# Graph attention in one sweep over 256 destinations

## The chip, the cores and the metric

One core of a Trainium2 chip runs the program once; the time is device microseconds of that execution. TensorE (PE) does matmuls and transposes, VectorE (DVE), ScalarE (ACT) and GpSimd (POOL) the elementwise work, SyncE (SP) issues DMAs. Tiles lie in SBUF or in PSUM (8 banks of 512 fp32 columns on 128 partitions), and the engines run apart from each other except for semaphores.

## The reference, cut to what matters

Four residual graph layers over 3125 nodes (padded to 3200 = 25 tiles of 128), 128 features and 103125 edges, each followed by a layer norm: a weighted sum with relu, the graph attention (GAT) that the change rewrites, a dot-product attention, and a two-layer mean aggregation. GAT, with 4 heads of 32 features and one self loop added per node:

```
h = (x @ W).reshape(n, HEADS, C)
a_s = jnp.einsum('nhc,hc->nh', h, att_src)
a_d = jnp.einsum('nhc,hc->nh', h, att_dst)
e = jax.nn.leaky_relu(a_s[src] + a_d[dst], NEG_SLOPE)      # slope 0.2
m = jax.ops.segment_max(e, dst, num_segments=n)
p = jnp.exp(e - m[dst])
z = jax.ops.segment_sum(p, dst, num_segments=n)
alpha = p / (z[dst] + EPS_SOFTMAX)
out = jax.ops.segment_sum(h[src] * alpha[:, :, None], dst, num_segments=n)
out = out.reshape(n, HEADS * C) + gat_bias + x @ skip_W + skip_b
```

## The kernel before

Edges are first turned into two dense 3200x3200 matrices in DRAM, rows by destination, columns by source: how often each edge occurs (`count_rs`) and the sum of its weights. `edge_tables` and `build_matrices` make them, `aggregate` and `finish_gcn` do the first layer; the change leaves these alone. Every stage is a block with its own engine programs, and the next block starts when all engines have left the one before. The order on each engine is written out by hand.

- `gat_project` computes h by head with a column of ones (`heads`), the attention terms per node (`cols`) and a_s and a_d as rows in DRAM (`rows_d`).
- `gat_max` goes over 25 tiles of 128 destinations. ScalarE sums a count tile for the degree (L941), turns it into a mask (L944, 0 where there is an edge, 1e30 where there is none) and takes its logarithm (L948). VectorE reduces a_s minus mask to a maximum for each of 4 heads (L983). TensorE turns the logarithms (L916, L917), ScalarE copies them out (L953), and they are stored as `log_sr`, rows by source.
- `gat_exponents` makes from the maximum the terms that each destination adds.
- `gat_attend` goes over the sources: 200 units of one head, one source tile and 1600 destinations. ScalarE adds a bias (L1157), VectorE takes the larger slope (L1189), then the minimum with 0 plus the log count (L1200), ScalarE raises (L1162), and TensorE gathers with the 33 columns of `heads` as stationary operand (L1214).
- `finish_gat` turns the sums back to nodes (L1272), adds each node's own loop (L1304, L1308), divides, adds the skip product, normalises twice, and turns X into XT (L485, L1295).
- `attend_rows` is the second attention, one tile of 128 destinations at a time: scores (L1435), masked minimum (L1526), Exp (L1493), times counts (L1540), turns (L1444), copies out of PSUM (L1498), gather (L1454). ScalarE masks the tile after next (L1487) in between.
- `mean_over_edges` runs twice over `log_sr`: ScalarE raises (L663), VectorE rounds to bf16 counts (L707), TensorE multiplies them with three bf16 parts of the features (L673). GpSimd copies the features (L609).

## Time and profile before

| what | us |
|---|---|
| median of 3 runs (3094.7 to 3097.13) | 3095.39 |
| the profiled execution's own time | 3097.05 |
| its span | 3095.4 |
| maximum to attend, 1108.2 to 2256.4 of the span | 1148.2 |

| | PE | DVE | ACT | POOL |
|---|---|---|---|---|
| busy us | 2427.7 | 2180.8 | 2119.9 | 579.5 |
| share of the span | 78% | 70% | 68% | 19% |

The shares are means over stages in which different engines are full, so the question for each stage is which engine never waits there. A group's row gives the busy time of its instructions as a union, their mean length, and the idle time just before them with what ended it. Two instructions on one engine can overlap, so busy time divided by the count can be less than the mean. An fp32 product leaves two MATMUL records, a transpose or a bf16 product one.

### The profile page before, as it was taken

To read this page: it belongs to the slowest core of one execution; us is meant where nothing else is said; L and a number is where in the kernel's file an instruction comes from. 1 tells how busy PE (TensorE), PEld (TensorE's weight loads), DVE (VectorE), ACT (ScalarE), POOL (GpSimd) and SP (SyncE) were. 2 spreads that over 40 slices of the span, in tenths; PEclk is the share of its full clock that TensorE was granted. 3 is DMA by queue.
4 is the path that set the end of the run, shared out by engine and by line. 5 is a ranking of instruction groups with operands and counts; after the bars stand their busy time and mean duration, and the time that the engine had idled before them with its cause. 6 is when DMAs were issued, how large, how long until landed. Compare 5 with 4: busy or idle time off the path is not lost. (4 is left out here: it accounts for less than half of the span.)

```text
span 3095.4 us, 52656 instructions
## 1 busy us (share of the span) xinstructions
PE 2427.7 (78%) x12244; PEld 1411.6 (46%) x12245; DVE 2180.8 (70%) x3601; ACT 2119.9 (68%) x3216; POOL 579.5 (19%) x950
## 2 busy tenths in 40 slices
PE   2898989999889556767488887888846999959785
PEld 1454445444445446656322222222244888845443
DVE  6777767777720249999699999999963555547165
ACT  2899989999940147777488888888824666637163
POOL 1444444444420000000011112111100000002020
PEclk7999999999999778888799999999967999979897
DMA  1222222222268047666511113111103333139093
GB/s 43 98 108 97 103 97 103 103 103 104 104 255 308 28 174 230 216 217 222 193 64 53 60 57 138 64 53 59 46 4 129 111 123 127 43 138 409 14 406 145
DMA packets 173354, 398.35 MB, mean 129 GB/s; under 512 B 7655, under 2 KB 147234, under 8 KB 156450
## 3 DMA queue, kind: packets, MB, share of 16 engines
q1 hardware_dynamic: 92698, 355.11, 31.1%
q10 hardware_dynamic: 80400, 40.96, 4.5%
q14 instruction: 233, 1.91, 0.2%
q8 instruction: 23, 0.38, 0.1%
HBM read 271.34 MB, written 124.70 MB: 128 GB/s over the span
## 5 line engine op out<-in xcount | busy, mean ns | idle before, releaser
L436 PE MATMUL ps_build<-OH,KEY 128*128 128x400 bf16 x4108 | 737.0, 339 | 82.5 <-ACT KEY L393 49.7
L393 ACT ACTIVATE KEY<-KEY,cols 128x128 bf16<-128x128 bf16 x2054 | 621.9, 397 | 98.5 <-DVE KEY L364 98.0
L1214 PE MATMUL ga_ps<-ga_p,ga_left 128*33 128x400 f32 x1600 | 567.9, 500 | 154.6 <-ACT ga_p L1162 154.6
L436 PEld LDWEIGHTS ps_build<-OH,KEY 128*128 128x128 bf16 x4108 | 399.7, 99 | 420.1 <-DVE OH L368 82.5
L364 DVE TENSOR_SCALAR KEY<-iota_key,key_base,cols 128x128 bf16<-128x128 int16 x1027 | 389.6, 412 | 219.5 <-PE ps_build L436 191.7
L411 POOL TENSOR_TENSOR KEY<-KEY,cols 128x256 bf16<-128x256 bf16 (+1 forms) x627 | 376.7, 601 | 497.8 <-DVE KEY L364 497.8
L1214 PEld LDWEIGHTS ga_ps<-ga_p,ga_left 128*33 128x33 f32 x1600 | 160.2, 110 | 562.2 <-issue 561.9
L1189 DVE SCALAR_TENSOR_TENSOR ga_p<-ga_u,att_cols,ga_p 128x1600 f32<-128x1600 f32 x201 | 376.6, 1874 | 20.2 <-ACT ga_p L1157 20.2
L1162 ACT ACTIVATE ga_p<-ga_p 128x1600 f32<-128x1600 f32 x200 | 307.3, 1536 | 95.0 <-DVE ga_p L1200 95.0
L983 DVE CUSTOM_DVE_ANT_0 gm_unread<-gm_src_rows,gm_closed 128x3200 bf16<-128x3200 f32 x100 | 343.3, 3488 | 39.2 <-ACT gm_closed L944 30.9
L1200 DVE SCALAR_TENSOR_TENSOR ga_p<-ga_p,ga_log 128x1600 f32<-128x1600 f32 x200 | 365.1, 1825 | 0.0
L1157 ACT ACTIVATE ga_p<-ga_u,att_cols 128x1600 f32<-128x1600 f32 x203 | 327.6, 1614 | 23.8 <-DMA ga_u<-gat_u_d 23.8
L1148 POOL COPY ga_left<-heads 128x33 f32 x200 | 135.5, 679 | 982.2 <-PE ga_ps L1214 571.0
L368 DVE TENSOR_SCALAR OH<-iota_low,cols 128x400 bf16<-128x400 int16 x1027 | 293.2, 317 | 0.0
L916 PE MATMUL gm_ps<-gm_minus,gm_closed 128*128 128x128 bf16 x625 | 149.9, 240 | 143.8 <-ACT gm_logs L953 120.9
L917 PE MATMUL gm_ps<-ident,gm_ring 128*128 128x128 f32 x1250 | 253.3, 340 | 0.0
L917 PEld LDWEIGHTS gm_ps<-ident,gm_ring 128*128 128x128 f32 x1250 | 223.4, 223 | 14.0
L673 PE MATMUL sage_ps<-sage_counts,sage_parts 128*128 128x400 bf16 x1200 | 206.7, 336 | 20.1 <-DVE sage_counts L707 20.1
L663 ACT ACTIVATE sage_ring<-sage_ring 128x3200 f32<-128x3200 f32 x50 | 143.5, 2871 | 62.7 <-DMA sage_ring<-log_count_by_source 62.6
L386 ACT ACTIVATE stage<-ps_build 128x800 f32<-128x800 f32 x201 | 166.2, 827 | 2.7 <-PE ps_build L436 2.6
L673 PEld LDWEIGHTS sage_ps<-sage_counts,sage_parts 128*128 128x128 bf16 x1200 | 118.3, 99 | 108.7 <-DVE sage_counts L707 21.2
L1526 DVE CUSTOM_DVE_ANT_0 ar_p<-ar_ps,ar_closed 128x1600 f32<-128x1600 f32 x50 | 91.1, 1823 | 106.1 <-PE ar_ps L1435 95.4
(287 smaller groups left out, 2414.7 us busy)
## 6 DMA issues: line engine op xcount, KB each, us to landing
adjacency<-stage SPq DMA_DIRECT2D x200, 400.0 KB, 2.5
sage_ring<-log_count_by_source SPq DMA_DIRECT2D x50, 1600.0 KB, 8.4
agg_gcn_ring<-adjacency SPq DMA_DIRECT2D x25, 1600.0 KB, 8.3
gm_ring<-adjacency SPq DMA_DIRECT2D x25, 1600.0 KB, 6.9
log_count_by_source<-gm_logs ACTq DMA_DIRECT2D x25, 1600.0 KB, 7.1
ga_log<-log_count_by_source SPq DMA_DIRECT2D x50, 800.0 KB, 4.3
ar_counts<-adjacency SPq DMA_DIRECT2D x25, 1600.0 KB, 6.7
ga_u<-gat_u_d SPq DMA_DIRECT2D x8, 1600.0 KB, 12.1
```

The source lines that it names most:

```text
L364: last = dve.tensor_scalar(KEY[:, slot + j, 0, :], k.iota_key[:, :], k.key_base[:, bass.ds(w, 1)], k.cols[:, 0, bass.ds(c + j, 1)], ALU.ad ...
L393: last = act.activation(KEY[:, slot + j, v, :], KEY[:, slot + j, 0, :], ACT.Copy, scale=k.cols[:, 1 + v, bass.ds(c + j, 1)])
L411: pool.tensor_tensor(KEY[:, slot:slot + n, 1, :], KEY[:, slot:slot + n, 0, :], k.cols[:, 2, bass.ds(c, n)].unsqueeze(2).to_broadcast([P, n ...
L436: last = pe.matmul(ps[:, 2 * (s % 2) + (v > 0), 0:SL], KEY[:, slot + j, v, :], OH[:, slot + j, :], start=slot == s % 2 * (BODY + 1) and j ...
L673: last = pe.matmul(ps[:, b, 0:CW], parts[:, u, i, :], counts[:, u, b * CW:(b + 1) * CW], start=False, stop=True, skip_group_check=True)
L917: last = pe.matmul(ps[:, b, c:c + P], ring[:, u, s * P:(s + 1) * P], k.ident[:], start=False, stop=True)
L983: dve.tensor_tensor_reduce(out=unread[:, h], in0=src_rows[:, h], in1=closed[:, u], scale=1.0, scalar=-3.0e38, op0=ALU.subtract, op1=ALU.ma ...
L1157: act.activation(p[:, slot, :], u[:, h, 1, :], ACT.Identity, bias=cols[:, HEADS + h, bass.ds(t, 1)]).then_inc(slopes, 1)
L1162: act.activation(p[:, i, :], p[:, i, :], ACT.Exp).then_inc(exps, 1)
L1189: dve.scalar_tensor_tensor(p[:, slot, :], u[:, h, 0, :], cols[:, h, bass.ds(t, 1)], p[:, slot, :], ALU.add, ALU.max).then_inc(larger, 1)
L1200: dve.scalar_tensor_tensor(p[:, slot, :], p[:, slot, :], 0.0, log[:, slot // HEADS, :], ALU.min, ALU.add).then_inc(scores, 1)
L1214: last = pe.matmul(ps[first:first + C + 1, h // 2 * HB + b, 0:CW], left[:, slot, :], p[:, slot, b * CW:(b + 1) * CW], start=False, stop=Tr ...
```

## The change

`gat_max`, `gat_exponents` and `gat_attend` become one function, `gat_rows`. It goes over 13 groups (`super_tile`) of 256 destinations, the last of 128, and in each over 4 heads: 52 units. GpSimd adds the self loops to the counts' diagonal blocks. The slope is split: e = 0.2(a_s + a_d) + max(0.8 a_s + 0.8 a_d, 0). For a unit VectorE has the masked maximum (`best`, two passes of 3125), four small steps (`level`), and `span`: for each of the two destination tiles `r = max(0.8 a_s + lift, floor)`, destinations on partitions. TensorE turns r in 50 blocks into 6 rotating PSUM banks, ScalarE raises each 128x256 block with the source's 0.2 a_s as bias (`power`), VectorE takes the minimum with 1 times the turned counts (`weigh`, 6400 columns in two parts), and TensorE gathers with 50 products of 33 stationary and 128 moving columns, the two destination tiles at PSUM partitions 0 and 64. One small product (`join`) turns a head's sums to nodes, and they go to DRAM (`node_d`). Counts are turned once per group by TensorE, copied by ScalarE and stored as `count_sr`.

`finish_gat` loads `node_d`, turns X first and no longer at its end; `attention_project` turns X instead and halves the copy between ScalarE and VectorE. The degrees are no longer a by-product of `gat_max`: ScalarE sums each count tile in `attend_rows` (`measure`), and `finish_attention` makes the reciprocal. `mean_over_edges` reads plain counts: no Exp, GpSimd subtracts the identity, VectorE casts.

```diff
+def gat_rows(nc, k, heads, cols, rows_d):
...
+            def turn_piece(g, h, i):
+                u = g * HEADS + h
+                if i == 0:
+                    pe.wait_ge(ranged, u + 1)
+                    need(pe, raised, u * PIECES)
+                    if h == 0:
+                        pe.wait_ge(taken_n, g * 5 + width(g))
+                    if h == 1:
+                        pe.wait_ge(taken_n, counts_done(g))
+                if i >= RINGS:
+                    pe.wait_ge(raised, u * PIECES + (i - RINGS + 1))
+                for s in range(i * BLOCKS, min(NT, (i + 1) * BLOCKS)):
+                    for j in range(width(g)):
+                        c = s % BLOCKS * WIDE + j * P
+                        last = pe.transpose(ps[:, i % RINGS, c:c + P], r[:, j, s * P:(s + 1) * P], k.ident[:])
+                last.then_inc(turned, 1)
...
+            def gather(g, h, s):
+                for j in range(width(g)):
+                    last = pe.matmul(ps[j * PAIR:j * PAIR + C + 1, 7, 0:P], heads[:, h, s, :], e[:, s, j * P:(j + 1) * P],
+                                     start=s == 0, stop=s == NT - 1, skip_group_check=True)
+                return last
...
+            def super_tile(g):
+                for h in range(HEADS):
+                    g0, h0 = (g, h - 1) if h else (g - 1, HEADS - 1)
+                    before = h > 0 or not is_super(g, 0)
+                    for i in range(RINGS):
+                        turn_piece(g, h, i)
+                    for i in range(RINGS, PIECES):
+                        if before:
+                            gather_chunk(g0, h0, i)
+                        turn_piece(g, h, i)
+                    if h == HEADS - 1 and not is_super(g, LAST):
+                        first_counts(g + 1)
+                    if before:
+                        join(g0, h0)
+                    gather_first(g, h)
+                    if h == 0:
+                        other_counts(g)
...
+            def power(g, h, i):
+                act.wait_ge(turned, (g * HEADS + h) * PIECES + (i + 1))
+                w = width(g) * P
+                for s in range(i * BLOCKS, min(NT, (i + 1) * BLOCKS)):
+                    c = s % BLOCKS * WIDE
+                    last = act.activation(e[:, s, 0:w], ps[:, i % RINGS, c:c + w], ACT.Exp, bias=cols[:, h, s:s + 1])
+                last.then_inc(raised, 1)
...
+            def span(g, h):
+                u = g * HEADS + h
+                need(dve, turned, u * PIECES)
+                dve.wait_ge(levelled, u + 1)
+                n = columns(g)
+                for j in range(width(g)):
+                    last = dve.tensor_scalar(r[:, j, 0:n], src_rows[:, h, 0:n], lift_u[:, h, j:j + 1],
+                                             floor_u[:, h, j:j + 1], ALU.add, ALU.max)
+                last.then_inc(ranged, 1)
+
+            def weigh(g, first, last):
+                w = width(g) * P
+                part = e[:, first:last, 0:w]
+                dve.scalar_tensor_tensor(part, part, 1.0, count_t[:, first:last, 0:w], ALU.min, ALU.mult
+                                         ).then_inc(weighed, 1)
...
+                for h in range(HEADS):
+                    span(g, h)
+                    if h:
+                        weigh_rest(g, h - 1)
+                    elif not is_super(g, 0):
+                        weigh_rest(g - 1, HEADS - 1)
+                    g2, h2 = next_best(g, h)
+                    if g2 is not None:
+                        best(g2, h2, 0)
+                    weigh_first(g, h)
+                    if g2 is not None:
+                        if width(g2) > 1:
+                            best(g2, h2, 1)
+                        level(g2, h2)
...
 def finish_gat
+            turn(pe, ps, k.X, k.ident[:]).then_inc(turned, 1)
             pe.wait_ge(copied, 1)
-            pe.wait_ge(loaded, 80)
-            project(pe, ps, [k.XT], [w[:]]).then_inc(projected, 1)
-            pe.wait_ge(x_ready, 1)
-            turn(pe, ps, k.X, k.ident[:]).then_inc(x_turned, 1)
+            pe.wait_ge(loaded, 96)
+            project(pe, ps, [XT], [w[:]]).then_inc(projected, 1)
...
 def attend_rows
+            def measure(t, u):
+                act.wait_ge(kept, t)
+                act.wait_ge(measured, t + RING)
+                act.activation(unread[:], counts[:, u, :], ACT.Copy, accum_out=deg_u[:, u % 2]).then_inc(measured, 1)
...
+                if exists(t, 2):
+                    measure(t + 2, (u + 2) % RING)
...
 def mean_over_edges
+                    pool.wait_ge(loaded[u], lap * 16 + 16)
+                    own = ring[:, u, bass.ds(t * P, P)]
+                    pool.tensor_tensor(own, own, k.ident[:], ALU.subtract).then_inc(opened, 1)
...
-                        dve.wait_ge(raised, t + 1)
-                        dve.tensor_scalar(counts[:, u, :], ring[:, u, :], ROUND, ROUND, ALU.add, ALU.subtract
-                                          ).then_inc(rounded, 1)
+                        dve.wait_ge(opened, t + 1)
+                        dve.tensor_copy(counts[:, u, :], ring[:, u, :]).then_inc(rounded, 1)
```

In the instruction order, VectorE in the attend stage before, two units (`ga_p` the exponents, `ga_u` the rows of destination terms, `ga_log` the log counts):

```order
L1188 REGISTER_ALU
L1189 ISA
L1189 SCALAR_TENSOR_TENSOR ga_p<-ga_u,att_cols,ga_p 128x1600
L1200 SCALAR_TENSOR_TENSOR ga_p<-ga_p,ga_log 128x1600
L1188 REGISTER_ALU
L1189 ISA
L1189 SCALAR_TENSOR_TENSOR ga_p<-ga_u,att_cols,ga_p 128x1600
L1200 SCALAR_TENSOR_TENSOR ga_p<-ga_p,ga_log 128x1600
```

And VectorE now, one unit of the first group of `gat_rows`, its second head:

```order
L1179 TENSOR_SCALAR gr_r<-gr_src_rows,gr_lift_u,gr_floor_u 128x3125 x2
L1186 SCALAR_TENSOR_TENSOR gr_e<-gr_e,gr_count_t 128x3328
L1152 ISA gr_unread,gr_best_u<-gr_src_rows,gr_closed 128x3125
L1152 ISA gr_best_u 128x1
L1186 SCALAR_TENSOR_TENSOR gr_e<-gr_e,gr_count_t 128x3072
L1152 ISA gr_unread,gr_best_u<-gr_src_rows,gr_closed 128x3125
L1152 ISA gr_best_u 128x1
L1162 TENSOR_TENSOR gr_peak<-gr_best_u,att_cols 128x2
L1164 SCALAR_TENSOR_TENSOR gr_peak<-gr_peak 128x2
L1167 SCALAR_TENSOR_TENSOR gr_floor_u<-gr_peak,att_cols 128x2
L1170 TENSOR_TENSOR gr_lift_u<-gr_floor_u,att_cols 128x2
```

The maximum, which had a stage of its own, now stands between the passes over the exponents, for the head after next; of the two passes with two tensors one is left, and the other is a pass with one tensor.

TensorE now, from the middle of a unit to the start of the next (`gr_r` is what is turned, `gr_e` what is gathered, `gr_out_t` what is joined); before, a unit was four products of 400 columns:

```order
L1019 MATMUL gr_ps<-gr_e,heads 33x128 x4
L990 MATMUL gr_ps<-ident,gr_r 128x128 x4
L1019 MATMUL gr_ps<-gr_e,heads 33x128 x4
L990 MATMUL gr_ps<-ident,gr_r 128x128 x4
L1019 MATMUL gr_ps<-gr_e,heads 33x128 x2
L990 MATMUL gr_ps<-ident,gr_r 128x128 x2
L1042 MATMUL gr_ps<-ident,gr_out_t 128x66
L1019 MATMUL gr_ps<-gr_e,heads 33x128 x24
L990 MATMUL gr_ps<-ident,gr_r 128x128 x24
```

Turns of one unit and products of the unit before now alternate in pieces.

ScalarE in the second attention now, from its mask to the copies of the next tile (line numbers of the changed kernel; before, the row of L1473 was not there):

```order
L1468 ACTIVATE ar_closed<-ar_counts,ar_big 128x3200
L1479 ACTIVATE ar_p<-ar_p,ar_low 128x1600 x2
L1483 REGISTER_ALU
L1484 ACTIVATE ar_pt<-ar_ps 128x512
L1483 REGISTER_ALU
L1484 ACTIVATE ar_pt<-ar_ps 128x512
L1483 REGISTER_ALU
L1484 ACTIVATE ar_pt<-ar_ps 128x512
L1483 REGISTER_ALU
L1484 ACTIVATE ar_pt<-ar_ps 128x128
L1472 REGISTER_ALU
L1473 ACTIVATE ar_unread,ar_deg_u<-ar_counts 128x3200
```

The degree's sum stands behind the last copy of a tile and ahead of the first copy of the next.

## Rows read from the trace of the kernel before

**Rows 1.** Busy time by stretch: maximum, attend, finish of GAT, second attention (columns named first).
```profile
core 0: us, PE busy (x) PEld busy (x) DVE busy (x) ACT busy (x) POOL busy (x), PEclk, DMA share, GB/s
...
1200.00:1500.00 300.00, 202.57 (x1496) 188.30 (x1496) 279.09 (x201) 227.31 (x98) 0.00 (x0) 0.84 0.67 213
...
1600.00:2200.00 600.00, 478.49 (x1354) 135.33 (x1352) 596.26 (x337) 516.48 (x338) 117.22 (x168) 0.99 0.21 68
...
2256.00:2338.00 82.00, 35.32 (x175) 34.56 (x175) 51.59 (x86) 16.75 (x35) 0.00 (x0) 0.56 0.02 4
...
2380.00:2700.00 320.00, 318.81 (x2113) 262.68 (x2111) 178.86 (x256) 214.24 (x232) 5.93 (x20) 1.00 0.30 108
```

**Rows 2.** Groups by line on VectorE: count, busy us, mean ns, idle before.
```profile
L1189 DVE SCALAR_TENSOR_TENSOR ga_p<-ga_u,att_cols,ga_p 128x1600 f32<-128x1600 f32 x201 | 376.6, 1874 | 20.2 <-ACT ga_p L1157 20.2
L1200 DVE SCALAR_TENSOR_TENSOR ga_p<-ga_p,ga_log 128x1600 f32<-128x1600 f32 x200 | 365.1, 1825 | 0.0
L983 DVE CUSTOM_DVE_ANT_0 gm_unread<-gm_src_rows,gm_closed 128x3200 bf16<-128x3200 f32 x100 | 343.3, 3488 | 39.2 <-ACT gm_closed L944 30.9 <-DVE deg L989 8.0 <-DMA gm_src_rows<-gat_rows_d 0.4
...
L243 DVE TENSOR_SCALAR pick<-win,cmin,cidx 128x200 f32<-128x200 f32 x7 | 2.7, 384 | 0.3
...
L217 DVE TENSOR_SCALAR src_hi<-src_f 128x896 f32<-128x896 f32 x1 | 0.6, 627 | 0.0
```

**Rows 3.** Groups by line on ScalarE, same columns.
```profile
L1498 ACT ACTIVATE ar_pt<-ar_ps 128x512 f32<-128x512 f32 x150 | 78.1, 591 | 79.1 <-PE ar_ps L1444 79.1
...
L941 ACT ACTIVATE gm_unread_act<-gm_ring 128x3200 bf16<-128x3200 f32 x25 | 71.8, 2871 | 83.9 <-DMA gm_ring<-adjacency 77.1 <-issue 6.0 <-ACT gm_logs L953 0.8
...
L1498 ACT ACTIVATE ar_pt<-ar_ps 128x128 f32<-128x128 f32 x25 | 7.0, 279 | 0.0
```

**Rows 4.** Groups by line on TensorE; two records stand for one fp32 product.
```profile
L1214 PE MATMUL ga_ps<-ga_p,ga_left 128*33 128x400 f32 x1600 | 567.9, 500 | 154.6 <-ACT ga_p L1162 154.6
```

**Rows 5.** Timeline of TensorE in the attend stage: start us, length us, then the group.
```profile
1700.45 2.85 PE L1214 MATMUL ga_ps<-ga_p,ga_left 128*33 128x400 f32 x8 [0.70 <-ACT ga_p L1162]
```

**Rows 6.** Timeline of one tile of the second attention.
```profile
2452.61 2.84 PE L1454 MATMUL ar_ps<-ar_pt,X 128*128 128x128 f32 x24
...
2455.28 1.47 PE L1444 MATMUL ar_ps<-ident,ar_p 128*128 128x128 f32 x12
...
2462.61 0.29 DVE L1548 COPY acc_t<-ar_ps 128x128 f32 x1 [0.52 <-PE ar_ps L1454]
2462.93 1.57 ACT L1498 ACTIVATE ar_pt<-ar_ps 128x512 f32<-128x512 f32 x3 [3.06 <-PE ar_ps L1444]
...
2466.30 2.84 PE L1454 MATMUL ar_ps<-ar_pt,X 128*128 128x128 f32 x24
...
2468.71 3.15 ACT L1493 ACTIVATE ar_p<-ar_p,ar_low 128x1600 f32<-128x1600 f32 x2 [1.36 <-DVE ar_low L1534]
```

**Rows 7.** Tile gm_ring: how long its loads took from issue to landing.
```profile
DMA to landing us min/median/max: 6.3/6.9/24.7
```

**Rows 8.** Timeline: SyncE's first load of the maximum stage.
```profile
1108.21 0.34 SPq L893 DMA_DIRECT2D gm_ring<-adjacency  x1
```

**Rows 9.** Timeline from the end of the attend stage to the second attention's projection.
```profile
2256.39 0.34 SPq L1260 DMA_DIRECT2D fg_w<-in_L_gnn_skip_W_dram  x1
...
2256.44 21.57 PE L1272 MATMUL fg_ps<-ident,head_sums 97*128 97x66 f32 x100 [3.18 <-PEq L1076]
...
2293.88 3.49 DVE L1316 TENSOR_TENSOR fg_t<-fg_t,fg_ps 128x3200 f32<-128x3200 f32 x1
...
2328.21 5.59 PE L485 MATMUL fg_ps<-ident,X 128*128 128x128 f32 x25 [38.59 <-DVEq L1321]
...
2340.48 7.54 PE L1347 MATMUL ap_ps<-XT,ap_wq 128*128 128x400 f32 x16 [6.67 <-DMA ap_wk<-in_L_gnn_Wk_dram]
```

**Rows 10.** Timeline of the start of the first mean over edges.
```profile
2766.30 2.87 ACT L663 ACTIVATE sage_ring<-sage_ring 128x3200 f32<-128x3200 f32 x1 [5.87 <-DMA sage_ring<-log_count_by_source]
...
2771.08 14.15 PE L673 MATMUL sage_ps<-sage_counts,sage_parts 128*128 128x400 bf16 x73 [9.23 <-DVE sage_counts L707]
```

More of the change, by code:

```diff
@@ new lines, in is_super, with width, columns, each_super @@
+        def is_super(g, which):
+            return isinstance(g, int) and g == which
+        def width(g):
+            return 1 if is_super(g, LAST) else TWO
+        def columns(g):
+            return NP if is_super(g, LAST) else N
+        def each_super(eng, work):
+            work(0)
+            with eng.Fori(1, LAST - 1) as g:
+                work(g)
+            work(LAST - 1)
+            work(LAST)
+        def next_best(g, h):
+            if h < TWO:
+                return g, h + TWO
+            return (None if is_super(g, LAST) else g + 1), h - TWO
@@ L889, in _, with counts_done @@
+        def counts_done(g):
+            return g * 5 + (2 * width(g) + 1)
         @block.sync
         def _(sp):
[L891 to L898 removed]
@@ L899, in _, with load, store_node @@
-            load(1, 1, 0)
-            with sp.Fori(1, NT // 2) as lap:
-                for u in range(2):
-                    load(lap * 2 + u, u, lap)
-            load(NT - 1, 0, NT // 2)
+            def load(g, j):
+                sp.dma_start(count[:, j, :].unsqueeze(1), rows[bass.ds(g * TWO + j, 1)].rearrange("t p c -> p t c")
+                             ).then_inc(loaded[j], 16)
+            def store_node(g, h):
+                n = width(g) * (C + 1)
+                hold(sp, kept, g * HEADS + (h + 1), held_sp)
+                sp.dma_start(k.node_d[:, h, bass.ds(g * (TWO * (C + 1)), n)], node[:, h % TWO, 0:n]
+                             ).then_inc(node_stored[h % TWO], 16)
@@ L1006, in gat_exponents, with finish_gat @@
+            for h in range(TWO):
+                for j in range(TWO):
+                    best(0, h, j)
+                level(0, h)
+            each_super(dve, super_tile)
+            weigh_rest(LAST, HEADS - 1)
+def finish_gat(nc, k):
     with ExitStack() as ctx:
```

678 lines of the change are left out of this document (296 added, 382 removed).

## The prediction

> **What bounds the kernel now.** I read the busy times by stretch first, to find the engine that never waits in each stage that the change touches [rows 1]. From 1200 to 1500 us (the maximum) VectorE is busy 279.09 of 300 us. From 1600 to 2200 (the attend stage) it is busy 596.26 of 600, TensorE 478.49 and ScalarE 516.48. So VectorE sets the time of both stages that are replaced, from the first load at 1108.21 [rows 8] to the first load of the next block at 2256.39 [rows 9]: 1148.2 us. The groups by line say what VectorE does there [rows 2]: 100 passes of 3200 for the maximum (343.3 us) and 401 passes of 1600 (376.6 and 365.1 us). In the second attention (2380 to 2700) TensorE is busy 318.81 of 320 [rows 1], so whatever makes TensorE wait there costs its full length. In the finish of GAT (2256 to 2338) no engine is full: a chain, read from the timeline [rows 9]. Below, a unit is one head of one group of 256 destinations, and T its period; 48 units have full width, 4 half.
>
> **VectorE's work in a unit.** A pass with two tensors costs 1.04 ns an element, from (3488 - 1825) / 1600, and 0.16 us fixed [rows 2]; queued behind another, 0.08 of that is hidden (337 instructions of mean 1.85 in 596.26 us, 1.77 each [rows 1, 2]).
> - Maximum: 343.3 / 100 is 3.43 us a pass of 3200, so 3.35 for 3125; two are 6.7 us. This work only moves: 100 passes before and after.
> - Minimum and times counts: 6400 elements in two passes, 6.67 + 2 x 0.08 = 6.8 us.
> - `span`, two passes with one tensor and two scalars per partition. No row has 3125 of them, so I bound it. A single-tensor pass of 896 took 627 ns, that is 0.52 ns an element over the same 0.16 us, half the price of two tensors. One of 200 with two such scalars took 384 ns, 0.10 + 0.28 [rows 2]. That gives 3125 x 0.52 + 0.28 = 1.9 us a pass, 3.6 for two with the overlap. The upper bound is full price, 3125 x 1.04 + 0.28 = 3.5 us a pass, or 3.1 us more a unit. I take 1.9: both rows with one tensor lie there (at full price 896 elements would have taken 1.09 us).
> - `level`: four tiny steps, each waiting for the one before: 0.9 us, the fixed 0.16 to 0.28 each.
>
> Together 18.0 us a unit. For all of the work that is some 930 us where the two stages had 1085.
>
> **TensorE's work in a unit.** At full clock (0.99 to 1.00 where TensorE was busy 80% and more [rows 1]) 24 records of 128 columns ran in 2.84 us, 12 turns in 1.47 us [rows 6]; less the last one's tail that is 0.111 us a record or turn, 0.222 a product. 50 turns are 5.55 us, 50 products 11.1, the join 0.2. That is 16.9, with 1.4 for a fourth of the count turns 18.3: the same as VectorE. To this come waits that the order forces. The join needs a copy that ScalarE makes after its last block, about 1 us after the last turn; for the last head the next group's counts are turned in that gap. After the first head, 26 count turns wait for a copy of 1536 columns (1.4 us), and the second head's turns wait for the last one. Head by head I get 21.7, 18.0, 18.0 (VectorE's) and 19.6 us, T = 19.3.
>
> ScalarE: 25 blocks of 256 between 279 ns (128 columns) and 591 ns (512) [rows 3], so about 0.38 us plus the bias, 25 x 0.46 = 11.5 at most; count copies 1.7, masks 1.5, the two small copies 0.5. Even at 591 ns a block it has 18.5 us, so it is hidden; if not, the sixth block comes late for `weigh_first`. GpSimd has only the diagonal adds. Loads: 6.9 us each [rows 7], two a group, due a unit later. The stores of counts and sums queue on SyncE behind the loads and have three units' time. If they blocked, the mask would be late and VectorE with it.
>
> **The stage.** At the start six transfers queue: 6.9 us for the first, some 4.1 for each further one (the longest landing, 24.7, was that of a load behind four others of its size [rows 7], part of it while the first was under way). So the second count tile is there at 15 us, its mask at 19, four passes and two levels follow, and the first `span` ends at 35. The last group is half wide, but its products are not paired and its first unit still gathers the wide one before: 46 us, and a tail of 8 with the sums' store. Narrow or missing passes take 10 off. So the stage takes 79 + 48 T = 1005 us against 1148.2: -143.
>
> **The rest.**
> - Finish of GAT: before, 21.57 us of products lie ahead of everything, and the add of the skip product starts 37.5 us after the block's start [rows 9]. Now the node sums (1.7 MB) and five small loads land at about 9.5 us, VectorE has 12.5 us of work, and TensorE (turns 5.6, copy 2.8, product 8.2) is done before it: 22. That is -15.5. X was turned and copied at the end, 2328.21 to 2336.7, then the next block's weights were waited for until 2340.48 [rows 9]. Now the turn covers that wait and the copy is halved: -3.3.
> - Second attention: the period is 2466.30 - 2452.61 = 13.69 us [rows 6]. The added sum of 2.87 us [rows 3] starts only when the tile's result is kept (2462.61 + 0.29), where ScalarE took the next tile's pieces at 2462.93. So it delays copies (1.6), mask (3.0) and Exp (3.15), and Exp starts at 8.0 of the period and not at 6.4. The fourth piece is then copied at 11.7, where TensorE wanted it at 10.7. TensorE waits, which it did not: 1.1 us a tile, 24 tiles, +26. Bounds: 0 if slack hides it, 2.9 a tile (+69) if all shows.
> - Means over edges: the first product waits for load, Exp (2.87) and rounding, 2766.30 to 2771.08 [rows 10]. Exp goes, a diagonal subtraction of some 0.7 us comes: -2 in each of the two, -4. Later TensorE is full.
> - Three scaled copies for one in the projection, and the degrees' steps ahead of an already waiting VectorE: +1.5.
>
> Sum: -143 - 19 + 26 - 4 + 1.5 = -138. From 3097.05 that is 2959, and as the median of the runs lies 1.7 lower, **2957 us**.
>
> **Rivals.**
> 1. *Products of the two destination tiles overlap.* They write PSUM partitions 0 and 64, in turn. In the trace products of one such place follow each other at 0.336 us a record [rows 5], two passes of 400 columns, and no unit alternates, so nothing speaks for or against. If pairs overlapped, 50 products took 5.6 us, VectorE alone would set T at about 18.4: 43 us less, 2915. TensorEngine Tiling (Array Packing), section Key Properties, of the Trainium skill says tiles "can execute LdWeights and Matmul in parallel", and one of 33 columns is such a half tile. No run here shows it. Chance 0.25.
> 2. *`span` at full price*, or ScalarE late: T = 21.1 to 21.5, 3045 to 3065. Against it: the row of 896. Chance 0.13.
> 3. *Each change between turns and products drains TensorE.* 14 changes a unit. The tail of a record is 0.5 - 0.336 = 0.164 us [rows 4, 5], a weight load's 0.111 more: 0.28 each, 3.9 a unit, T = 23.2, stage 1193: **3144 us, slower**. It decides from T = 22.2, that is 0.2 us a change. Against it: in the second attention turns and products alternate four times a tile and TensorE still does 16 + 50 records and 25 turns in 13.69 us, no more than the 13.7 that their rates add up to [rows 6]; but those fill the whole array. The same Key Properties say that changing the tiling mode drains TensorE, which would hold here and not there; no row shows it. With the tail alone (2.3 a unit) the time is 3067. Chance of the slower end 0.10, of the tail alone 0.1.
> 4. *Nothing is gained*, the new stage ends as long as the two old: T near 22.2. Chance 0.02, the same.
>
> The forecast, T from 18.9 to 20.3 (2940 to 3005), has 0.40. The range 2895 to 3070 takes in rival 1, rival 2 and the tail alone, and the second attention's bounds; 0.2 is left out, mostly the slow end. Of 3095 us 0.2% is 6 us, about what a measurement of this kernel can tell: faster 0.88, same 0.02, slower 0.10.
>
> **What would show it.** In the changed profile: the new stage 1005 us long, VectorE busy about 93% of it and TensorE as much; `span` passes of 1.9 us; `ar` periods of 14.8 us with a wait of TensorE for ScalarE's copies; the add of the skip product 22 us after its block's start. Wrong if a `span` pass takes 3.5 us, if turns after products start later than 0.1 us, or if ScalarE is what VectorE waits for.

## The result and the profile after

The changed kernel took **2929.93 us** (median of 4 runs, 2928.34 to 2930.75); the kernel before took 3096.26 us (4 runs) beside it. The ratio is 0.9459, 95% interval 0.9447 to 0.947: faster by 5.4%. The forecast was 2957 us, 27 us too long, with the time inside its range of 2895 to 3070. Two kernels of the experiments ran once each well above their other five executions (6160.44 us at a granted clock of 1.0, and 3041.42 us at 0.806 where the others had 0.926 to 0.93), and the times given for them below are the medians of the five. The profiled execution took 2929.37 us, 167.7 less than that of before. Where the 167.7 us went, by the starts of the same instructions in both traces:

| part | before, us | after, us | difference | forecast |
|---|---|---|---|---|
| up to the first load of the replaced stages | 1108.2 | 1106.6 | -1.6 | 0 |
| replaced stages, to the first load of the finish of GAT | 1148.2 | 985.4 | -162.8 | -143 |
| finish of GAT, to the first projection | 84.1 | 63.9 | -20.2 | -18.8 |
| second attention with its projection, to the last acc_t copy | 378.1 | 397.4 | +19.3 | +26 (and part of the +1.5) |
| finish of the attention | 40.7 | 41.4 | +0.7 | part of the +1.5 |
| means over edges, to the end | 336.1 | 333.0 | -3.1 | -4 |

In the busy time by stretch, against [rows 1]: the new stage stands in the first line, the second attention in the second.

```profile
core 0: us, PE busy (x) PEld busy (x) DVE busy (x) ACT busy (x) POOL busy (x), PEclk, DMA share, GB/s
1200.00:1900.00 700.00, 586.40 (x6151) 462.52 (x6152) 668.24 (x447) 487.67 (x1075) 34.13 (x18) 0.96 0.25 86
2240.00:2540.00 300.00, 290.35 (x1868) 228.44 (x1866) 156.26 (x244) 244.94 (x247) 5.04 (x17) 1.00 0.27 97
```

VectorE is busy 95% of the new stage, as it was 93 and 99% of the two old ones; ScalarE has become idle for 30% of it. TensorE's 586 us look like much, but this is time in which some record was under way; the record rates below tell more. The second line is the cost: TensorE was busy 318.81 of 320 us in the second attention and is now idle 3% of it.

The groups by line of the page, in place of [rows 2] and [rows 4]:

```profile
L990 PE MATMUL gr_ps<-ident,gr_r 128*128 128x128 f32 x2500 | 389.0, 296 | 100.2 <-DVE gr_r L1179 86.6
...
L1019 PE MATMUL gr_ps<-gr_e,heads 128*33 128x128 f32 x5000 | 364.9, 277 | 25.5 <-DVE gr_e L1186 25.5
L1186 DVE SCALAR_TENSOR_TENSOR gr_e<-gr_e,gr_count_t 128x3072 f32<-128x3072 f32 (+1 forms) x104 | 349.5, 3361 | 36.1 <-ACT gr_count_t L1100 23.4
L1152 DVE CUSTOM_DVE_ANT_0 gr_unread<-gr_src_rows,gr_closed 128x3125 bf16<-128x3125 f32 (+1 forms) x100 | 344.4, 3444 | 19.6 <-DMA gr_src_rows<-gat_rows_d 15.2
...
L1179 DVE TENSOR_SCALAR gr_r<-gr_src_rows,gr_lift_u,gr_floor_u 128x3125 f32<-128x3125 f32 (+1 forms) x100 | 186.7, 1907 | 11.1 <-PE gr_ps L990 6.2
```

A `span` pass takes 1.907 us (1.9 in the forecast), and VectorE's work in a unit is 18.2 us (18.0). TensorE is what the forecast had wrong. Its timeline, a whole group of 256 destinations first, then the half-wide last one:

```profile
1510.62 2.81 PE L1019 MATMUL gr_ps<-gr_e,heads 128*33 128x128 f32 x48
...
1518.02 0.63 PE L1019 MATMUL gr_ps<-gr_e,heads 128*33 128x128 f32 x8 [0.53 <-DVE gr_e L1186]
1518.59 0.66 PE L990 MATMUL gr_ps<-ident,gr_r 128*128 128x128 f32 x4
1519.17 0.63 PE L1019 MATMUL gr_ps<-gr_e,heads 128*33 128x128 f32 x8
...
2071.91 2.81 PE L1019 MATMUL gr_ps<-gr_e,heads 128*33 128x128 f32 x24
```

In the last group, with one destination tile, 24 records take 2.81 us, 0.11 us each, as forecast. In a whole group, where the products of two tiles alternate, 48 records take the same 2.81 us. A product costs 0.111 us and not 0.222. The rows between show the changes: 8 records of products start 0.57 us before the 4 turns behind them, the 4 turns 0.585 us before the next products, where their rates alone give 0.444 each. A change costs 0.13 us.

TensorE's clock is not full everywhere in this stage. Its busy time and granted clock, first while VectorE makes the `span` passes of a third head, then over the 24 turns behind them, in two parts, and last over the 24 turns of the next group's first head (columns us, PE busy (x), PEclk, DMA share, GB/s):

```profile
1474.30:1477.70 3.40, 0.00 (x0) 0.86 1.08 386
1477.74:1480.50 2.76, 2.76 (x13) 0.50 0.63 216
...
1514.66:1517.49 2.83, 2.83 (x24) 1.00 0.00 0
```

TensorE had nothing to do for 3.44 us, and behind that the granted clock was 0.50, its lower level (1.2 GHz), so that 24 turns took 5.38 us and not 2.83. Four groups further, after the same 3.44 us, the 24 turns at 1778.60 took 2.83 us. Both heads were 18.23 us long, so the slower clock cost nothing: VectorE did not wait for it.

What VectorE still waits for is in the second head of each group. The starts of the `span` passes are 18.22, 20.16, 18.23 and 18.60 us apart in a regular group. Their mean is T = 18.80 us (forecast 19.3). The timelines of TensorE, ScalarE and VectorE around the long one:

```profile
1526.82 2.81 PE L1019 MATMUL gr_ps<-gr_e,heads 128*33 128x128 f32 x48
1529.56 2.84 PE L999 MATMUL gr_ps<-ident,gr_count 128*128 128x128 f32 x24
1532.63 0.44 PE L999 MATMUL gr_ps<-ident,gr_count 128*128 128x128 f32 x2 [0.23 <-ACT gr_count_t L1096]
```

```profile
1531.13 2.79 ACT L1096 ACTIVATE gr_count_t<-gr_ps 128x1536 f32<-128x1536 f32 x2 [4.73 <-PE gr_ps L999]
1533.81 0.39 ACT L1100 ACTIVATE gr_count_t<-gr_ps 128x256 f32<-128x256 f32 x1
```

```profile
1534.23 3.63 DVE L1186 SCALAR_TENSOR_TENSOR gr_e<-gr_e,gr_count_t 128x3328 f32<-128x3328 f32 x1 [1.57 <-ACT gr_count_t L1100]
```

The first head's products run first, then the count turns, then ScalarE copies, and VectorE, 1.57 us idle, needs the last copy.

The finish of GAT, against [rows 9]: the add of the skip product starts 21.2 us after the block's first load (22 forecast), where it had stood at 37.5, and the projection's first product at 63.9.

```profile
2092.01 0.35 SPq L1250 DMA_DIRECT2D fg_node<-gat_node_sums  x1
...
2113.17 3.49 DVE L1285 TENSOR_TENSOR fg_t<-fg_t,fg_ps 128x3200 f32<-128x3200 f32 x1
...
2155.89 4.31 PE L1319 MATMUL ap_ps<-XT,ap_wq 128*128 128x400 f32 x7 [1.97 <-ACT XT L1325]
```

The second attention, against [rows 6]: from one group of 24 records to the next are 14.63 us where there were 13.69 (forecast 14.8). Over all 24 intervals of the acc_t copies it is 343.4 us against 324.4, +19.0. The timelines of TensorE, ScalarE and VectorE:

```profile
2287.01 2.94 PE L1434 MATMUL ar_ps<-ar_pt,X 128*128 128x128 f32 x24
...
2294.35 0.33 PE L1424 MATMUL ar_ps<-ident,ar_p 128*128 128x128 f32 x1 [0.40 <-ACT ar_pt L1484]
...
2301.64 2.94 PE L1434 MATMUL ar_ps<-ar_pt,X 128*128 128x128 f32 x24
```

```profile
2283.51 2.87 ACT L1473 ACTIVATE ar_unread<-ar_counts 128x3200 bf16<-128x3200 f32 x1 [2.70 <-DVE acc_t L1540]
```

```profile
2292.33 1.83 DVE L1530 CUSTOM_DVE_ANT_0 ar_p<-ar_p,ar_counts 128x1600 f32<-128x1600 f32 x1 [3.16 <-ACT ar_p L1479]
```

ScalarE sits idle for 2.70 us until VectorE has kept the tile's result, and only then starts the sum of 2.87 us.

### The profile page after: what moved, and what is told of

It is laid out like the page before. It is cut to its first block and busy times, and to the rows that moved or that the text cites. A ratio compares the mean times of both kernels' runs of the same rounds, so it can differ in the third digit from the quotient of the medians.

```text
span 2927.7 us, 62500 instructions
## 1 busy us (share of the span) xinstructions
PE 2393.8 (82%) x16906; PEld 1621.4 (55%) x16907; DVE 2007.1 (69%) x3577; ACT 1787.0 (61%) x4164; POOL 476.1 (16%) x825
## 5 line engine op out<-in xcount | busy, mean ns | idle before, releaser
L1083 ACT ACTIVATE gr_e<-gr_ps,att_cols 128x256 f32<-128x256 f32 (+1 forms) x1300 | 502.0, 485 | 212.5 <-PE gr_ps L990 210.0
L990 PE MATMUL gr_ps<-ident,gr_r 128*128 128x128 f32 x2500 | 389.0, 296 | 100.2 <-DVE gr_r L1179 86.6
L990 PEld LDWEIGHTS gr_ps<-ident,gr_r 128*128 128x128 f32 x2500 | 291.4, 150 | 183.8 <-issue 136.9
L1019 PE MATMUL gr_ps<-gr_e,heads 128*33 128x128 f32 x5000 | 364.9, 277 | 25.5 <-DVE gr_e L1186 25.5
L1186 DVE SCALAR_TENSOR_TENSOR gr_e<-gr_e,gr_count_t 128x3072 f32<-128x3072 f32 (+1 forms) x104 | 349.5, 3361 | 36.1 <-ACT gr_count_t L1100 23.4
L1152 DVE CUSTOM_DVE_ANT_0 gr_unread<-gr_src_rows,gr_closed 128x3125 bf16<-128x3125 f32 (+1 forms) x100 | 344.4, 3444 | 19.6 <-DMA gr_src_rows<-gat_rows_d 15.2
L1019 PEld LDWEIGHTS gr_ps<-gr_e,heads 128*33 128x33 f32 x5000 | 255.1, 111 | 93.0 <-issue 54.9
L1179 DVE TENSOR_SCALAR gr_r<-gr_src_rows,gr_lift_u,gr_floor_u 128x3125 f32<-128x3125 f32 (+1 forms) x100 | 186.7, 1907 | 11.1 <-PE gr_ps L990 6.2
L1415 PE MATMUL ar_ps<-KT,ar_left 128*128 128x400 f32 x400 | 146.9, 511 | 14.0 <-DVE ar_low_u L1516 12.5
L1434 PE MATMUL ar_ps<-ar_pt,X 128*128 128x128 f32 x1250 | 150.2, 277 | 1.1
## 6 DMA issues: line engine op xcount, KB each, us to landing
count_by_source<-gr_count_t SPq DMA_DIRECT2D x12, 3200.0 KB, 18.7
```

The lines of the kernel that those rows point to most:

```text
L990: last = pe.transpose(ps[:, i % RINGS, c:c + P], r[:, j, s * P:(s + 1) * P], k.ident[:])
L1019: last = pe.matmul(ps[j * PAIR:j * PAIR + C + 1, 7, 0:P], heads[:, h, s, :], e[:, s, j * P:(j + 1) * P], start=s == 0, stop=s == NT - 1, s ...
L1083: last = act.activation(e[:, s, 0:w], ps[:, i % RINGS, c:c + w], ACT.Exp, bias=cols[:, h, s:s + 1])
L1152: dve.tensor_tensor_reduce(out=unread[:, 0:n], in0=src_rows[:, h, 0:n], in1=closed[:, j, 0:n], scale=1.0, scalar=FLOOR, op0=ALU.subtract, ...
L1186: dve.scalar_tensor_tensor(part, part, 1.0, count_t[:, first:last, 0:w], ALU.min, ALU.mult).then_inc(weighed, 1)
L1434: last = pe.matmul(ps[:, 7, 0:P], k.X[:, first + j, :], pt[:, i, j * P:(j + 1) * P], start=first + j == 0, stop=first + j == NT - 1, skip_ ...
```

## The experiments

**Theory**: VectorE's passes set the period of three heads in four. TensorE would have been as long but for its pairs of products running side by side. The second head ends by the chain of the count copies, and the 19 us lost in the second attention come from where the added sum stands. **Rivals**: a product is cheap whatever its neighbour; TensorE's chain sets the pace; the sum costs its own length wherever it is. Gains are given against the changed kernel's 2929.93 us. The kernel before, run beside each set on its chip, took 3097.0, 3096.86 and 3096.64 us.

### Pairs of products apart

```diff
-            def gather(g, h, s):
+            def gather(g, h, blocks):
                 for j in range(width(g)):
-                    last = pe.matmul(ps[j * PAIR:j * PAIR + C + 1, 7, 0:P], heads[:, h, s, :], e[:, s, j * P:(j + 1) * P],
-                                     start=s == 0, stop=s == NT - 1, skip_group_check=True)
+                    for s in blocks:
+                        last = pe.matmul(ps[j * PAIR:j * PAIR + C + 1, 7, 0:P], heads[:, h, s, :],
+                                         e[:, s, j * P:(j + 1) * P],
+                                         start=s == 0, stop=s == NT - 1, skip_group_check=True)
```

> The products of a chunk are issued tile by tile (all its blocks for destinations 0 to 127, then all for 128 to 255) instead of in turns; same products, same number of changes between turns and products. Theory A: the two tiles' products overlap on TensorE because neighbours in the queue use different halves of the array, which is why a record took 0.0555 us in the whole groups and 0.111 us in the last, single one. Then the records go back to 0.111 us, a head's 50 products cost 11.1 us instead of 5.55, TensorE has 18.9 us of work a head plus its hand-offs and becomes the bound: a head takes 20 to 21 us instead of 18.5, and the kernel 70 to 120 us more, 3000 to 3050 us. Rival B: a product is simply cheaper than I took it, whatever its neighbour: records stay at 0.0555 us and the time within 3 us of 2930.

Measured: 2964.32 us, +34. The timeline of TensorE in this kernel (products are line 1020):

```profile
1500.21 0.64 PE L1020 MATMUL gr_ps<-gr_e,heads 128*33 128x128 f32 x8
1500.78 0.66 PE L990 MATMUL gr_ps<-ident,gr_r 128*128 128x128 f32 x4
...
1504.42 5.02 PE L1020 MATMUL gr_ps<-gr_e,heads 128*33 128x128 f32 x48
```

The long run of 24 and 24 records went from 2.81 to 5.02 us, so the overlap is real and the rival falls. But the short runs, now 4 and 4, kept their 0.57 us: neighbours need not alternate one by one. So TensorE lost only 2.2 us a head, and just the second head was long enough for it to show: 18.23, **22.77**, 18.23 and 18.6 us. 12 times 2.6 is 31 of the 34 us. My expectation of 70 to 120 took all records to lose the overlap.

The same trace shows how far apart two records may stand and still overlap. TensorE in three stretches of 0.44 us of that long run: among the records of the first tile, at the change to the second, among the records of the second (same columns as above; a record under way at an edge of a stretch is counted):

```profile
1505.60:1506.04 0.44, 0.44 (x6) 1.00 0.34 75
1506.63:1507.07 0.44, 0.44 (x10) 1.00 0.00 0
1508.20:1508.64 0.44, 0.44 (x7) 1.00 0.00 0
```

The clock is full in all three, so it is not what made the run longer. Record by record, the starts are 0.109 us apart, but the first 4 records of the second tile start beside the last 4 of the first, and so it is in all 48 long runs of this trace. Four of 24 records overlap, and 44 times 0.109 with the last one's tail make the 5.02 us. Runs of 4 and 4 overlap whole by the same measure.

### Fewer changes between turns and products

```diff
-                    for i in range(RINGS, PIECES):
-                        if before:
-                            gather_chunk(g0, h0, i)
-                        turn_piece(g, h, i)
+                    for first in range(RINGS, PIECES, 2):
+                        two = range(first, min(PIECES, first + 2))
+                        for i in two:
+                            if before:
+                                gather_chunk(g0, h0, i)
+                        for i in two:
+                            turn_piece(g, h, i)
```

> TensorE changes half as often between turns and products after the ring is full: two chunks of products, then two pieces of turns. Theory A (VectorE sets the pace): a change's 0.13 us is paid on an engine with room, so within 4 us of 2930, though TensorE's own turns-and-products stretch gets shorter by 0.5 to 0.8 us a head. Rival B (TensorE's chain sets the pace): 0.6 to 0.8 us a head less, 30 to 38 us faster, about 2895. Rival C: the later turns starve ScalarE and the next weigh pass comes late: 10 to 30 us slower.

Measured: 2920.81 us (2919.17 to 2921.78), -9. TensorE's timeline:

```profile
1517.98 1.07 PE L1019 MATMUL gr_ps<-gr_e,heads 128*33 128x128 f32 x16 [0.52 <-DVE gr_e L1189]
1518.98 1.09 PE L990 MATMUL gr_ps<-ident,gr_r 128*128 128x128 f32 x8
1520.00 1.07 PE L1019 MATMUL gr_ps<-gr_e,heads 128*33 128x128 f32 x16
```

16 records and 8 turns take 2.02 us, where twice 8 and 4 took 2 x 1.15: 0.28 less for two changes saved, the 0.13 to 0.14 us a change again. The heads that VectorE sets did not move (18.22, 18.23, 18.6); the second went from 20.16 to 19.63 us, some 6 us in all, and the narrow last group gave 2. Neither theory had that: A holds for three heads, B for the second.

### A shorter VectorE pass

```diff
-                weigh(g, CUT, NT)
+                weigh(g, CUT, CUT + 5)
```

> Leaves out part of the computation: the second 'minimum times counts' pass covers 5 of its 13 source blocks, so the edges of the last 8 blocks are summed without their counts. Theory A: VectorE sets the pace of the graph attention (busy 18.2 of 18.5 us a head). The pass falls from 3.44 to about 1.35 us, a head from 18.5 to 16.4 to 16.8 us, the kernel by 80 to 100 us to 2830 to 2850, and TensorE's granted clock stays near 1. Rival B: TensorE and ScalarE's chain (turn, Exp, turn) is just as long and a head keeps 18 us or more: at most 25 us gained, above 2905.

This kernel leaves out the counts of 8 of the 25 source blocks. Measured: 2878.7 us, -51, between the two. The pass fell from 3.62 to 1.48 us, 2.1 us a head or 107 us in all, and half of it came through. The heads took 16.98, 19.2 to 19.4, 16.8 to 17.9 and 17.17 us. VectorE sets the pace, but 0.8 to 1.4 us behind it stands the next chain. What VectorE waited for in this kernel between 1200 and 1900 us (us in total, times, longest):

```profile
DVE gr_e L1186 <- ACT gr_e L1083: 30.7, 40, 2.2
...
DVE gr_e L1186 <- ACT gr_count_t L1100: 22.2, 10, 2.2
```

The first did not exist in the changed kernel in this stretch: ScalarE's Exps, which TensorE's turns feed.

### The sum of the second attention earlier

```diff
-                act.wait_ge(kept, t)
+                if not isinstance(t, int) or t > 1:
+                    act.wait_ge(kept, t - 1)
...
-                act.activation(unread[:], counts[:, u, :], ACT.Copy, accum_out=deg_u[:, u % 2])
+                act.activation(unread[:], counts[:, u, :], ACT.Copy, accum_out=deg_u[:, u])
```

> Second attention: ScalarE's sum of a tile's counts no longer waits for the tile's own results to be kept, but for the tile's before, so it can run in ScalarE's idle time before the tile's end. Theory A: the period rose from 13.69 to 14.63 us because the sum (2.87 us) stands between keep and the next tile's Exp and VectorE waits behind it. With it earlier the period returns to 13.7 to 13.9 us: 15 to 19 us less, 2911 to 2915. Rival B: ScalarE's chain is full and the 2.87 us cost the same wherever they stand: within 4 us of 2930. Rival C: the sum now delays Exp pieces of the next tile itself and costs 5 to 20 us more.

Measured: 2911.76 us (2906.54 to 2915.59), -18, where A had 15 to 19 less. ScalarE's timeline (the sum is now line 1474, Exp line 1480):

```profile
2277.38 3.15 ACT L1480 ACTIVATE ar_p<-ar_p,ar_low 128x1600 f32<-128x1600 f32 x2 [1.35 <-DVE ar_low L1525]
...
2282.12 2.86 ACT L1474 ACTIVATE ar_unread<-ar_counts 128x3200 bf16<-128x3200 f32 x1
...
2291.06 3.15 ACT L1480 ACTIVATE ar_p<-ar_p,ar_low 128x1600 f32<-128x1600 f32 x2 [1.35 <-DVE ar_low L1525]
```

The sum starts without idle time before it, the period is 13.68 us again, and the 24 intervals take 324.4 us, what they took before the change. The sum of 2.87 us is free in the place where ScalarE was idle; all of the 19 us came from the wait ahead of it: theory A.

### The counts before the products

```diff
-                    gather_first(g, h)
                     if h == 0:
                         other_counts(g)
+                    gather_first(g, h)
...
                 for s in range(CUT):
+                    if h == 0 and s == CUT // 2:
+                        last_counts(g)
                     gather(g, h, s)
```

> After a group's first head TensorE turns the second half of the counts before the first products of that head and the last block of counts half way through them, instead of both behind the 2.81 us of products. Theory A: of each group only the second head waits, for the last copy of the counts (VectorE 1.57 us idle there and the head 20.16 us instead of 18.2), because that chain starts late. The copies now end 2.2 us or more earlier, the head falls to 18.2 to 18.4 us, 12 groups give 20 to 24 us: 2906 to 2910. Rival B: what makes that head longer is the amount of ScalarE's or TensorE's work in it, not its order: under 6 us gained.

Measured: 2909.12 us (2907.79 to 2910.19), -21. The timelines of TensorE, ScalarE and VectorE (count copies are lines 1100 and 1104, the pass line 1190):

```profile
1519.12 2.79 PE L999 MATMUL gr_ps<-ident,gr_count 128*128 128x128 f32 x24
1521.83 1.50 PE L1021 MATMUL gr_ps<-gr_e,heads 128*33 128x128 f32 x24
```

```profile
1520.63 2.79 ACT L1100 ACTIVATE gr_count_t<-gr_ps 128x1536 f32<-128x1536 f32 x2 [1.84 <-PE gr_ps L999]
1523.74 0.38 ACT L1104 ACTIVATE gr_count_t<-gr_ps 128x256 f32<-128x256 f32 x1 [0.32 <-PE gr_ps L999]
```

```profile
1524.96 3.62 DVE L1190 SCALAR_TENSOR_TENSOR gr_e<-gr_e,gr_count_t 128x3328 f32<-128x3328 f32 x1
```

The last copy now ends before VectorE wants it, and the 1.57 us idle are gone; the second head takes 18.50 us instead of 20.16. Same work, another order: theory A.

### The levels on GpSimd

```diff
-                dve.tensor_tensor(peak[:, part], best_u[:, part], cols[:, HEADS + h, at], ALU.add).then_inc(small, 1)
+                pool.tensor_tensor(peak[:, part], best_u[:, part], cols[:, HEADS + h, at], ALU.add).then_inc(small, 1)
...
+                if j == 0 and (not isinstance(done, int) or done):
+                    hold(dve, levelled, done, held)
```

> The small steps of 'level' (a level and a floor per destination) go from VectorE to GpSimd; max(x, x/5) is written there as -x/4 - max(x, 0) under the factor -5/4, the same value. Theory A (VectorE sets the pace of three heads in four, the counts' chain that of the fourth): VectorE loses 0.9 us a head, the three heads fall from 18.2 to 18.6 us to 17.3 to 17.7, the fourth keeps its 20.2 since its chain ends at the counts: 0.9 x 3 x 12 = 32 us less, 2895 to 2901. Rival B: what VectorE does between its long passes is hidden somewhere else: within 5 us of 2930. Rival C: GpSimd's hand-offs or its share of the memory port slow VectorE's passes: 2935 or more.

Measured: 2931.59 us, no gain, where A had 2895 to 2901. The timelines of GpSimd and of VectorE in this kernel:

```profile
1512.16 1.62 POOL L979 TENSOR_TENSOR gr_peak<-gr_best_u,att_cols 128x2 f32<-128x2 f32 x1 [10.47 <-DVE gr_best_u L1186]
1513.97 5.19 POOL L981 TENSOR_SCALAR gr_fifth<-gr_peak 128x2 f32<-128x2 f32 x1 [0.20 <-POOL gr_peak L979]
1519.13 0.22 POOL L982 TENSOR_SCALAR gr_peak<-gr_peak 128x2 f32<-128x2 f32 x1
```

```profile
1511.82 3.72 DVE L1196 TENSOR_SCALAR gr_r<-gr_src_rows,gr_lift_u,gr_floor_u 128x3125 f32<-128x3125 f32 x2
1515.46 3.62 DVE L1203 SCALAR_TENSOR_TENSOR gr_e<-gr_e,gr_count_t 128x3328 f32<-128x3328 f32 x1
1520.74 3.42 DVE L1186 CUSTOM_DVE_ANT_0 gr_unread<-gr_src_rows,gr_closed 128x3125 bf16<-128x3125 f32 x1 [1.67 <-POOL gr_lift_u L989]
```

A step of two numbers a partition takes 0.20 us on GpSimd while VectorE is idle. Beside VectorE passes it lasts until one of them ends: 1512.16 + 1.62 is the end of the first `span` pass. The second step began beside the second `span` pass, but missed its end at 1515.54, where the weigh pass followed at once, and came to 1513.97 + 5.19 = 1519.16, the end of the weigh pass (1519.08). VectorE's next maximum pass then waited 1.67 us for the levels, since it writes the buffer that they read: more than the 0.9 us saved. Of the rivals C named the cause, though not VectorE's passes became slower, but GpSimd. Page SBUF — State Buffer of the Trainium skill, section Who interferes with whom, says that a GpSimd instruction which reads SBUF fully blocks behind a VectorE instruction that holds the shared port pair. By that rule the ends fall together, and the trace agrees, with 0.05 to 0.08 us between them.

### All four edits, with one buffer

> All four edits that left the result alone: fewer changes, the early sum, the levels on GpSimd, the counts before the products. Theory A: VectorE at 17.3 us sets every head; fewer changes then gives only its 2 to 3 us in the last group, early sum 18, levels 0.9 x 4 x 12 = 43, counts 22: 83 to 88 us less, 2842 to 2847. Rival B: behind VectorE stands the chain through TensorE and ScalarE at 17.2 us a head and 19.2 in the second one (the periods with the short pass), and it lets only a part through: 2855 to 2875.

Measured: 2907.23 us, and both theories missed it by 32 us or more. They had been written without the result of the run above, and this kernel carries the same wait (59.4 us of VectorE waiting for the levels between 1200 and 1900 us, heads of 18.7 to 19.4 us).

### Two buffers for the maxima

```diff
-        best_u = sb("gr_best_u", [P, TWO])
+        best_u = sb("gr_best_u", [P, TWO, TWO])
...
-                done = g * HEADS + h
+                done = g * HEADS + (h - 1)
```

> The levels on GpSimd as before, but with two buffers for the maxima, so that VectorE's next maximum pass no longer waits for GpSimd. In the run before GpSimd's small steps lasted until the end of whatever long VectorE pass ran beside them (1.62, 1.65, 3.57, 5.19 us for 128x2 numbers) and VectorE then waited 1.6 us a head for the last one, more than the 0.9 us it had saved. Theory A: that wait was the whole of it; now three heads of four take 17.3 to 17.6 us, the second keeps 20 us, and the kernel takes 28 to 36 us less than the changed kernel: 2894 to 2902. Rival B: GpSimd is held by each pass in turn, six steps do not end within a head, and the wait only moves to the span pass: 2920 or more. Rival C: TensorE's and ScalarE's chain stands right behind VectorE (17.2 us with the short pass) and takes half the gain: 2905 to 2915.

Measured: 2900.04 us, -30: theory A. The heads took 17.11 to 18.1, 19.2 to 20.2, 17.4 and 17.3 to 18.1 us. With a head's time to spare, GpSimd's slow steps cost VectorE 8.6 us between 1200 and 1900 and not 47.8. A buffer, not the engine's speed, had decided.

### Products apart, in longer chunks

This is the edit of the pairs apart together with that of the fewer changes.

> Products tile by tile as in the first run, in chunks of twice the size: 8 records for one half of the array, then 8 for the other. There 4 and 4 still took 0.57 us (as in turns), 24 and 24 took 5.02 us instead of 2.81. Theory A: weights are loaded a few records ahead, so a short row for one half still overlaps with the next half's: 8 and 8 take between 1.07 (all overlapped) and 1.8 us (none), about 1.4. Theory B: it is a matter of which half comes next only for long rows (something else is short in the 48): 8 and 8 take 1.07 us as in turns. The time: 2950 to 2970 us by A; the second head of each group stays near 22.5 us.

The edit did not do what was expected of it. Two chunks now follow each other, but each of them still has 4 records for one half and then 4 for the other, so that 16 records come as 4, 4, 4 and 4. No run has 8 and 8.

Measured: 2954.04 us (a single execution), 10 us less than the first run, about what fewer changes gave by themselves. In TensorE's timeline the 16 records start 1.02 us before the 8 turns behind them, against 1.00 where the two tiles alternate one by one: all of them overlap, as 4 and 4 did before. The long run, 24 and 24, takes 5.02 us and has its 4 overlapping records here too, and the second head takes 21.9 us. So neither theory was tested. The 4 records of the long runs let one expect that 8 and 8 would overlap in part, which is A's side, but that is not shown, nor is why the overlap ends there.

### Three edits without GpSimd, and all four

> Three edits without GpSimd: fewer changes, the early sum, the counts before the products. They act in different places, except that fewer changes and counts first both shorten the second head's wait (1.9 us in all): 18 for the sum, 21 for the counts, 2 to 4 for what fewer changes still give in the last group: 2886 to 2890 us. Rival: they overlap more than that, or the earlier turns come at the price of later Exps: 2893 or more.

Measured: 2886.93 us (2884.61 to 2887.4), -43, inside its range.

> All four edits, the levels with two buffers. Theory A: VectorE at 17.3 to 17.6 us sets all four heads: 2840 to 2852 us. Rival C (the chain through TensorE and ScalarE is nearly as long, in the second head above all): 2855 to 2870. Rival B (GpSimd late for the span pass): above 2885.

Measured: 2849.71 us, -80: theory A. The ratio to the kernel before is 0.92, 95% interval 0.9188 to 0.9211, so this version beats both. Its replaced stage takes 919.8 us (985.4 in the changed kernel). Heads take 17.27, 17.27, 17.97 and 17.11 us. The timelines of GpSimd and VectorE in it:

```profile
1513.59 3.10 POOL L984 TENSOR_TENSOR gr_peak<-gr_peak,gr_fifth 128x2 f32<-128x2 f32 x1 [0.19 <-POOL gr_peak L982]
1516.95 3.02 POOL L986 TENSOR_TENSOR gr_floor_u<-gr_peak,att_cols 128x2 f32<-128x2 f32 x1 [0.26 <-POOL gr_peak L984]
```

```profile
1513.23 3.41 DVE L1193 CUSTOM_DVE_ANT_0 gr_unread<-gr_src_rows,gr_closed 128x3125 bf16<-128x3125 f32 x1
...
1516.56 3.35 DVE L1210 SCALAR_TENSOR_TENSOR gr_e<-gr_e,gr_count_t 128x3072 f32<-128x3072 f32 x1
```

GpSimd mostly gets one step done per VectorE pass, whether maximum or weigh pass, and six of them fill about a head. VectorE is busy 691.04 of 700 us: little is left to take from its waits, only from its passes.

## Why the prediction was right, and where it was off

The direction and the mechanism held: two stages in which VectorE hardly waited were replaced by one with less VectorE work. That the time came as close as 1% is in part luck. The cost of a product was wrong by a factor of two, and it mattered little only because VectorE's 18.0 us a unit stood right beside TensorE's 18.3: halving the products could take no more off T than the waits above VectorE's work. The time also lies below the band of 2940 to 3005 us that the forecast gave the largest chance, on the side of rival 1. By the prediction's own steps:

- **VectorE's work in a unit**, 18.0 us: right, 18.2. (The "some 930 us" for all of it is too much by its own terms, 48 units of 18.0 and 4 of half that being 900; nothing rests on it.) The price of a `span` pass, taken from two rows with one tensor, was right to 0.01 us; rival 2 (full price) falls with it.
- **TensorE's work, "0.222 a product"**: this is the step that failed. A product costs 0.111 us, since pairs overlap: 50 cost 5.6 us and not 11.1. The row it rested on [rows 6] is of products that fill the whole array, and could not show it. Rival 1 named this case, with a chance of 0.25, and 2915 us, 15 us below the measured time where the forecast is 27 above. By the rule that it cites (TensorEngine Tiling (Array Packing), section Key Properties, of the Trainium skill: tiles run independently) products overlap; the trace agrees, with 0.0555 us a record against 0.11 in the half-wide group.
- **The waits on top, T = 19.3, head by head 21.7, 18.0, 18.0 and 19.6**: measured 20.16 for the head with the counts and 18.2 to 18.6 for the others, T = 18.80. The place of the long head was right (it is the chain over the count copies), its size 1.5 us too large. Of the last head's 1.6 us only 0.4 came, with the pairs apart too; that part of the step was wrong by itself. With the pairs apart in the long runs the heads took 18.2, 22.8, 18.2 and 18.6 us, 19.46 on average, and the kernel 2964 us. That is near the forecast, but not its kernel: 26 of the 50 products still overlapped there, and the whole excess is in one head. Rival 1's T of 18.4 was 0.4 too short, as it left the wait for the last count copy out: 0.4 x 48 is 19 us, the last group's 4 come on top, and the second attention gave 7 back: 2931.
- **Rival 3**, a price for each change: there is one, but smaller, and no run shows whether it is a drain. A change costs 0.13 us, less than the tail alone (0.164), and 14 of them lie on an engine with room: bringing them from 14 to 8 gave 9 us, 8 of them from the second heads and the last group. The prediction named more than 0.1 us a change as a sign that it was wrong; that sign came, but by its own reckoning the outcome turns only at 0.2.
- **The stage, 79 + 48 T**: the first `span` ended at 35.0 us (35); narrow and missing passes took off 10.4 (10); last group and tail came to 58.3 and not 54, which I have not taken apart. With T the stage is 985.4 and not 1005: -24 from T, +4 from the end.
- **Finish of GAT**, -18.8: right, -20.2.
- **Second attention**, +26: +19.0. The sum does stand where it was put, behind the keep, and the time comes from there (the earlier sum gave 18 us back). The term of 1.1 us a tile was sized at the fourth piece; the regular period rose 0.94, and over all 24 intervals it is 0.79.
- **Means**, -4: -3.1. **Small steps**, +1.5: +0.7 in the finish of the attention, 0.3 in the projection with the first tile.

The sum of the misses: -20 in the stage, -7 in the second attention, the rest under 3. One sum of the prediction does not close: the chances that it names inside its range of 2895 to 3070 add up to 0.88, which leaves 0.12 out and not 0.2.

## What to carry to other kernels

Before a product is priced by rows of full-array products, ask whether a neighbour in the queue writes another half: within 4 records of each other two such products cost what one does, and the gain reaches the time only in the stretch where TensorE's chain ends last. Where an operation is added to an engine with idle time, what it waits for counts more than how long it takes: the same 2.87 us cost 19 us behind a late wait and nothing ahead of it. Small steps moved to GpSimd need a buffer and a head's time to spare, as each lasts until a VectorE pass beside it ends.

## What the runs showed of the hardware

- Products of 33 columns into PSUM partitions 0 and 64 overlap: 0.0555 us a record in turns and in runs of 4 and 4. In runs of 24 and 24 only the last 4 records of one half and the first 4 of the other overlap, in all 48 such runs, and the 48 records take 5.02 us in place of 2.81. Runs between 4 and 24 were not measured.
- A change between turns (full array) and such products costs TensorE 0.13 us, each way.
- Behind 3.44 us without work TensorE's granted clock was 0.50 in one group and 24 turns took 5.38 us; in another group, behind 3.44 us too, 24 turns took 2.83 us.
- A GpSimd step on 128x2 numbers takes 0.20 us alone. Beside VectorE passes of two tensors, or of one tensor and two scalars, it ends 0.05 to 0.09 us after a pass does: mostly the pass that it began beside, now and then only the second or third, so that it takes 1.6 to 8.5 us (8.51 with two buffers, the levels alone). VectorE's passes beside it keep their length (3.44 us for the maximum, 1.92 for a `span` pass where it was 1.91).
